# Convolution matmuls of a two-layer network split from 64 to 32 output channels per matmul

## The reference, cut to what matters

```
x = x + conv3x3(group_norm(x), w2d[b])       # layer 0
x = x + circular_conv3x3(group_norm(x), L1)  # layer 1
```

## Time and profile before

| | us |
|---|---|
| median of 3 runs (1729.54 to 1730.8) | 1730.13 |
| profiled execution, its own time | 1728.56 |
| its span, first to last instruction | 1726.8 |
| TensorE busy | 1630.3 (94%) |
| DVE busy | 1294.9 (75%) |
| ACT busy | 1144.3 (66%) |
| GpSimd busy | 112.0 (6%) |

### The profile page before, as it was taken

The page is one execution under the profiler, slowest core; times in us unless marked ns, Lnnn a source line. Parts: engine busy times, 40 slices in busy tenths (PEclk is TensorE's granted clock), DMA queues, the critical chain, the costliest instruction groups (busy, mean ns, idle before and its releaser), DMA issues.

```text
span 1726.8 us, 63815 instructions
## 1 busy us (share of the span) xinstructions
PE 1630.3 (94%) x28906; PEld 1260.8 (73%) x28906; DVE 1294.9 (75%) x1744; ACT 1144.3 (66%) x1029; POOL 112.0 (6%) x347
## 2 busy tenths in 40 slices
PE   5888888789899999999999999999999999999999
PEld 4787778655467777887688778867786778677766
DVE  5999899889977777777777777777777777777600
ACT  6888878589666666666666666666666666666444
POOL 0000000031100020002000200020002000100100
PEclk9999999989999999999999999999999999999999
DMA  9999999935466566666666666666666665665255
GB/s 386 421 421 422 422 422 421 379 92 161 119 199 211 201 198 211 210 201 198 213 207 201 198 212 208 200 199 211 210 200 198 209 212 185 213 206 204 112 203 203
DMA packets 99668, 409.99 MB, mean 237 GB/s; under 512 B 16883, under 2 KB 17384, under 8 KB 83048
## 3 DMA queue, kind: packets, MB, share of 16 engines
q1 hardware_dynamic: 98025, 405.94, 65.7%
q0 software_dynamic: 672, 0.08, 0.1%
q10 hardware_dynamic: 735, 0.37, 0.1%
HBM read 271.83 MB, written 134.50 MB: 235 GB/s over the span
## 4 chain that ended last, share of the span: by engine, by line
PE 75%; DVE 12%; issue 7%; ACT 4%; DMA 2%; DVEq 0%; ACTq 0%; SPq 0%; POOL 0%; POOLq 0%
PE ps L527 72%; DVE x L810 9%; ACT x L633 2%; DMA x<-x_pix 1%; ACT x L668 1%; ACT x L670 1%; DMA x<-wf 1%; DVE x L1013 1%; DVE x L864 1%; DVE stats L1030 1%; PE ps L452 1%; PE ps L453 0%; ACT x L674 0%; PE ps L456 0%; PE ps L463 0%
## 5 line engine op out<-in xcount | busy, mean ns | idle before, releaser
L527 PE MATMUL ps<-x,wc 64*64 64x512 f16 x24540 | 1339.9, 377 | 10.3 <-DVE x L1013 9.4
L527 PEld LDWEIGHTS ps<-x,wc 64*64 64x64 f16 x24540 | 992.7, 107 | 351.5 <-issue 21.4
L864 DVE SCALAR_TENSOR_TENSOR x<-xin,gnp,x 128x1028 f16<-128x1028 f32 x247 | 320.3, 1298 | 234.6 <-ACT x L633 234.5
L633 ACT ACTIVATE x<-xin,gnp 128x1028 f16<-128x1028 f32 x247 | 286.4, 1160 | 307.6 <-PE ps L527 302.4
L684 ACT ACTIVATE outb<-ps,bias 128x1024 f32<-128x1024 f32 x256 | 285.3, 1114 | 155.0 <-PE ps L527 155.0
L1013 DVE SCALAR_TENSOR_TENSOR x<-ps,gnp,x 128x1024 f16<-128x1024 f32 x256 | 325.1, 1270 | 24.3 <-ACT x L670 24.0
L452 PE MATMUL ps<-x 128*128 128x129 f16 x2048 | 254.1, 224 | 59.0 <-DVE x L810 58.6
L810 DVE SCALAR_TENSOR_TENSOR x<-x 128x2048 bf16<-128x2048 f32 x128 | 282.8, 2283 | 19.3 <-DMA x<-wf 17.4
L1030 DVE BATCH_NORM_STATS2 stats<-ps 128x6 f32<-128x512 f32 x440 | 283.6, 687 | 11.1 <-ACT x L674 8.5
L619 ACT ACTIVATE x<-x 128x2048 f16<-128x2048 f32 x128 | 240.1, 1908 | 52.6 <-PE ps L453 36.0
L452 PEld LDWEIGHTS ps<-x 128*128 128x128 f16 x2048 | 197.7, 98 | 78.6 <-DVE x L810 78.6
(11 more groups left out here) (144 smaller groups left out, 292.2 us busy)
## 6 DMA issues: line engine op xcount, KB each, us to landing
x<-x_pix SPq DMA_DIRECT2D x128, 1024.0 KB, 11.5
out<-outb SPq DMA_DIRECT2D x256, 512.0 KB, 3.7
xin<-x_tiles SPq DMA_DIRECT2D x239, 514.0 KB, 3.6
xin<-x_tiles SPq DMA_DIRECT2D x8, 642.5 KB, 4.1
x<-x_tiles SPq DMA_DIRECT2D x9, 514.0 KB, 7.2
w<-taps_scratch SPq DMA_DIRECT2D x60, 8.0 KB, 2.7
w<-taps_scratch SPq DMA_DIRECT2D x30, 16.0 KB, 3.1
taps_scratch<-x POOLq DMA_DIRECT2D x21, 3.0 KB, 1.8
```

What stands on the lines that cost most here:

```text
L527: return nc.tensor.matmul(to.rearrange("p (r w) -> p r w", w=NCOL), lhs, two, start=first, stop=last)
L633: nc.scalar.activation(planes[:, 0, a:a + w], x_at(g), ACT.Identity, scale=gnp[:, 1, b:b + 1]).then_inc(hi0_ready, 1)
L864: V.scalar_tensor_tensor(planes[:, 1, a:a + w], x_at(g), gnp[:, 1, b:b + 1], planes[:, 0, a:a + w], ALU.mult, ALU.subtract).then_inc(lo0_r ...
```

## The change

In `quarter` a new argument `part` picks 32 of the 64 columns of the weights and 32 of the 64 output partitions. The loop that issued two matmuls (one for each kind) now issues four (each kind by each part). The moving operand, the bank, the flags, the order of the steps, the waits and what raises a semaphore stay as they were, except that the last of the four matmuls raises it. TensorE then works as eight tiles of 64 rows by 32 columns.

```diff
-            def quarter(layer, i, n, job, k, half, kind, q, first, last):
+            def quarter(layer, i, n, job, k, half, kind, part, q, first, last):
...
-                lhs = (wc0 if layer == 0 else wc1)[rows, (i // NCH) % 2, whl, kind, dj, :]
+                lhs = (wc0 if layer == 0 else wc1)[rows, (i // NCH) % 2, whl, kind, dj, 32 * part:32 * part + 32]
                 a, z = row_at(layer, i, n, r) + dj, row_at(layer, i, n, r + 1) + dj
-                to = ps[64 * kind:64 * kind + 64, bank, :]
+                lane = 64 * kind + 32 * part
+                to = ps[lane:lane + 32, bank, :]
...
-                    for kind in range(2):
-                        done = quarter(layer, i, chunk_of(job), job, k, half, kind, q, half == 0 and k == 0,
+                    for kind, part in itertools.product(range(2), range(2)):
+                        done = quarter(layer, i, chunk_of(job), job, k, half, kind, part, q, half == 0 and k == 0,
                                        half == 1 and k == len(PASSES) - 1)
```

More of the change, by code:

```diff
@@ L1 @@
+import itertools
 import math
```

## The result

The changed kernel takes 2007.49 us (median of 4 runs, 1998.64 to 2011.04) against 1730.05 (1729.54 to 1730.8): a ratio of 1.1596, 95% interval 1.1556 to 1.1635. It is slower by 277 us. The prediction of no change was wrong, and the time lies above the range (1727 to 1975). The profiled execution of the changed kernel is its slowest of the four (2011.04 us), so the profiles stand 282 us apart.

What follows compares the result with a forecast made beforehand. TensorE's convolution matmul stream was taken to bound the kernel; all terms were 0 over 6,144 steps, so the forecast was 1731 us, the 1730.13 median with 1 us for extra starts, range 1727 to 1975.

Steps and rivals of the forecast that it cites:

- (1): Convolution steps on TensorE: eight streams run together as four do, so a step stays 216.7 ns; change 0.
- R2: Rival, chance 0.10: column groups share their stream of moving data, a step takes 433.4 ns, 3061 us in all.
- (2): Convolution weight loads: 49,152 of 32 columns lie beside the matmuls, cost 0; without that cover +657 us.
- (3): TensorE's queue: 16 instructions a step, one per 13.5 ns, taken as 0; other end +517 us.
- the far form of the first rival: TensorE's queue: a 25 ns floor for each instruction, loads too, makes a step 400 ns, +1,126 us.
- (4): TensorE's instruction queue: a 256-instruction fetch needed every 3.47 us, taken as 0; one at a time, +51 to +243 us.
- (5): Semaphore waits between engines in the convolutions: in time nothing moves, and DVE's 24% slack absorbs a slightly later matmul.
- R1: Rival, chance 0.25: instruction supply at TensorE's queue bounds; by fetch 1781 to 1973 us, by decode up to 2247.
- R3: Rival, chance 0.12: it works, but extra starts take a little of each tile's time; 1735 to 1751 us.
- R4: Rival, chance 0.06: faster, as narrower weight loads free 3.4 ns a step or restarts are quicker; all of it 1709 us.
- the signs named ahead: Convolution trace: if right, 960 loads per 26 us; if supply bounds, fewer, with idle "issue" time or gaps ending with a fetch.

Runs made afterwards that it cites:

- the bare loop: Convolution matmul stream alone on eight 64 x 32 tiles, as an engine loop of 768 instructions, layers' arithmetic and other engines' work left out: 1346.68 us.
- the kernel with all matmuls cut: Kernel before the change, 64 x 64 tiles kept, every convolution matmul cut in two of 256 moving elements: 1978.71 us, ratio 1.1431.
- run 64: Not a label but a count of turns: the eight-tile stream as an engine loop with its body lengthened to 96 steps, 96 KB, 64 turns: 1347.01 us.

## Why the prediction was wrong, step by step

- What bounds the kernel before: right. TensorE's stream sets the pace, and a step is 216.7 ns.
- (1) Array time, 0: right. Between gaps eight tiles take 216.7 ns a step, in the kernel and in the bare loop. R2 is refuted.
- (2) Weight loads, 0: right. They take 93 ns beside the stream.
- (3) Issue, 0: right. The bare loop hands on an instruction in 13.5 ns for 1.3 ms. So the far form of the first rival, the 25 ns of the Trainium skill (TensorE: Matmul & The Clock Gate, section "Wait — 56ns, not 53.3ns?") taken for each instruction, loads too, does not hold here. Counted over matmuls alone the mean is 27.1 ns, which does not contradict the skill's figure; only the burst across tiles does, four matmuls started within 0.04 us.
- (4) **Instruction fetch, taken as 0: this is the step that failed.** It had the rival's conditions in it ("if only one is under way at a time") and priced it at +51 to +243 us. It measured 282 us in the profiled execution, above the upper end, since that end took the time from issue to landing of a data load, 4.1 us. The block's real distance is 4.26 us in the mean: 1.0 of packet, 1.4 until its first instruction, and 1.7 in the median until the next packet starts. That the guess of 4.1 us comes near this sum is luck.
- What made me choose 0 was the Gram loop, which runs without a fetch: "at least 64 KB of code are held at once, four fetches' worth". The fact is right, and even 96 KB are held. The conclusion is wrong: what is held of a loop says nothing on how far ahead a straight program is fetched. The 7 us between fetches in the trace before were set by the stream's use, so they showed that 6.9 us are enough, and nothing under that. What that trace did show, had each packet been paired with its block, is that each starts only around the first instruction of the block before it. The 1.4 us and the 1.1 us it could not show, as no block was late there.
- (5) The waits, no change: right. DVE's and ACT's longer waits are for the late matmuls.
- The rivals: R1 happened, in its fetch part; I gave it 0.25, and the prices of its fetch part ended at 1973 us, 34 us short. R3 and R4 did not.
- Of the signs named ahead, fewer than 960 loads in 26 us with idle "issue" time before the loads, and gaps that end with a fetch, are what the trace shows.

Open: why a packet is not fetched earlier, what the 1.1 us ahead of its start are spent on and why data transfers stretch them, and why the kernel with all matmuls cut loses 29 us less than the one with eight tiles (its cut step is longer, which leaves each fetch more time, but this was not tried by itself).

## What to carry to other kernels

Count the instructions of a straight-line program per microsecond, not only their durations: here TensorE could take one in 13.5 ns from a loop, but written out it got 256 in 3.6 us on a quiet chip and in 4.3 us beside half-busy data transfers, and 5.5 us beside full ones. A change that doubles instructions at the same array time pays nothing until that supply is reached and then pays for every block; a loop on the engine whose body is held (96 KB here) did not pay at all. And keep one tile width in a stream: two widths in each step made this kernel four times as slow.

## What the runs showed of the hardware that was not expected

- Instruction blocks of 16 KB for TensorE come one at a time, about one ahead of the block that runs and no further: about 1.0 us of packet (1.2 in the median of the quiet intervals that a gap ends), 1.4 us until its first instruction starts, and 1.1 us (quiet) to 3.2 us (full data traffic) until the next packet starts. Data traffic stretches only the last part.
- Eight tiles of 64 x 32 stream 512 columns in 216.7 ns, as four of 64 x 64, beside 411 GB/s of loads as well (26 us with 968 loads). A loop of 96 KB was fetched once, six packets, and then run 64 times.
- Changing between tiles of 64 and 32 columns twice a step makes a step 1.11 us instead of 0.22, and TensorE was granted 1.2 GHz nearly all the time (mean clock 0.522).
- 1.2 GHz was granted for 3.4 us three times behind the fetch gaps of the changed kernel, in a stage that ran at full clock before.
